# Perceiver megakernel on one core: in self attention, ScalarE copies one of four score banks to SBUF and GpSimd subtracts its maximum

## The reference

```
q = (X @ Wq.T + bq).reshape(b, s, N_KV, g, HEAD_DIM)      # 8 x 4 heads of width 8
k = (X @ Wk.T + bk).reshape(b, s, N_KV, HEAD_DIM)
v = (X @ Wv.T + bv).reshape(b, s, N_KV, HEAD_DIM)
scores = einsum('bkgqd,bkld->bkgql', q, k) / sqrt(HEAD_DIM)
weights = softmax(scores)                                   # over 64 keys
out = einsum('bkgql,bkld->bkgqd', weights, v)
x = x + out @ Wo.T + bo
```

## Time and profile before

| | |
|---|---|
| time, median of 3 runs | 3079.71 us (3079.54 to 3079.81) |
| the profiled execution, its time | 3095.65 us |
| the profiled execution, its span | 3093.9 us |
| granted TensorE clock over the span | 0.963 of full speed |
| busy, TensorE matmul | 2728.1 us (88%) |
| busy, VectorE | 1893.3 us (61%) |
| busy, ScalarE | 1381.1 us (45%) |
| busy, GpSimd | 1025.4 us (33%) |

### The profile page before, as it was taken

The page is one execution under the profiler, slowest core; times in us unless marked ns, Lnnn a source line. Parts: engine busy times, 40 slices in busy tenths (PEclk is TensorE's granted clock), DMA queues, the critical chain, the costliest instruction groups (busy, mean ns, idle before and its releaser), DMA issues. The chain is left out here.

```text
span 3093.9 us, 51159 instructions
## 1 busy us (share of the span) xinstructions
PE 2728.1 (88%) x19360; PEld 1711.5 (55%) x19364; DVE 1893.3 (61%) x2524; ACT 1381.1 (45%) x2650; POOL 1025.4 (33%) x868
## 2 busy tenths in 40 slices
PE   7999987999989988899989775578988899898898
PEld 5999953466656557333356432235643555554687
DVE  3666646222268637444478597768854899996332
ACT  3332343122257646222257553446767566652223
POOL 1222200233135322000045300015610899991462
PEclk9999999999999999999999887789999999999999
DMA  4000005111200000200000000000011112213224
GB/s 156 21 27 20 17 7 196 41 47 47 74 21 2 23 1 2 85 1 0 22 2 2 15 0 0 0 22 2 2 42 37 58 73 75 70 46 112 65 82 147
DMA packets 77016, 128.94 MB, mean 42 GB/s; under 512 B 12112, under 2 KB 54736, under 8 KB 76304
## 3 DMA queue, kind: packets, MB, share of 16 engines
q1 hardware_dynamic: 67888, 101.78, 9.9%
q0 software_dynamic: 8928, 24.39, 2.5%
HBM read 107.40 MB, written 18.74 MB: 41 GB/s over the span
## 5 line engine op out<-in xcount | busy, mean ns | idle before, releaser
L3433 POOL TENSOR_TENSOR h<-ssm_u,ss_bc 128x1024 f32<-128x1024 f32 x88 | 205.8, 2360 | 0.0
L3396 ACT ACTIVATE ssm_p_h<-ss_delta,ss_decay 128x256 f32<-128x256 f32 x352 | 146.6, 463 | 123.9 <-DVE ctxT L3470 82.9
L3343 PE MATMUL ssm_p_y<-ctxT,ident 128*128 128x512 f32 x412 | 187.8, 596 | 0.0
L3465 DVE TENSOR_TENSOR_SCAN ssm_p_h<-ssm_p_h,h 128x1024 f32<-128x1024 f32 x64 | 145.9, 2279 | 8.7 <-ACT ssm_p_h L3396 6.8
L683 POOL TENSOR_TENSOR xw_prob<-xw_prob,xw_rsum 128x512 f32<-128x512 f32 x64 | 65.3, 1041 | 259.1 <-DVE xw_rsum L632 259.1
L3423 POOL TENSOR_TENSOR ctxT<-ctxT,ss_bc 128x1024 f32<-128x1024 f32 x50 | 117.6, 2360 | 19.3 <-DVE ctxT L3463 19.3
L514 PE MATMUL xw_p_q<-h,xw_m_h 128*128 (+1 forms) x1024 | 119.7, 278 | 1.3 <-PEq L60 1.3
L514 PEld LDWEIGHTS xw_p_q<-h,xw_m_h 128*128 128x128 f32 x1024 | 116.6, 193 | 7.0 <-issue 7.0
L3343 PEld LDWEIGHTS ssm_p_y<-ctxT,ident 128*128 128x128 f32 x412 | 76.5, 192 | 79.5 <-issue 78.3
L3327 PE MATMUL ssm_p_h<-ssm_b_diagonal,ssm_uT 128*128 128x128 f32 x640 | 82.9, 284 | 39.9 <-DVE ctxT L3470 19.5
L522 PE MATMUL xw_p_q<-xw_u,xw_vo_h 128*128 128x128 f32 x1024 | 117.1, 275 | 1.2 <-ACT xw_u L586 1.2
(11 more groups left out here) (863 smaller groups left out, 7143.7 us busy)
## 6 DMA issues: line engine op xcount, KB each, us to landing
ss_bc<-ss_bc_rows SPq DMA_DIRECT2D x24, 896.0 KB, 4.3
xw_ctx_rows<-in_ctx_rows SPq DMA_DIRECT2D x32, 256.0 KB, 2.6
ss_bc<-ss_bc_rows SPq DMA_DIRECT2D x8, 768.0 KB, 4.0
L3f_rows<-L3f_rows_out SPq DMA_DIRECT2D x16, 384.0 KB, 4.0
L0f_wg<-in_L_ffn_gate SPq DMA_DIRECT2D x9, 512.0 KB, 9.4
L0f_wu<-in_L_ffn_up SPq DMA_DIRECT2D x9, 512.0 KB, 9.4
L0f_wd<-in_L_ffn_down SPq DMA_DIRECT2D x9, 512.0 KB, 9.5
L0f_rows<-L0f_rows_out SPq DMA_DIRECT2D x16, 256.0 KB, 3.9
```

Of the source, the lines that this page charges most:

```text
L3343: mm = pe.matmul(p_y[:, 2 * half:2 * half + 2, :].rearrange("p e t -> p (e t)"), k.ident[:, :], weighed[n % RING_W][:, ts(half, CH)], star ...
L3396: i = act.activation(out[:, ts(e, CT)], delta[:, e, ts(c, CT)], ACT.Exp, scale=decay[:, E4 * s + e:E4 * s + e + 1])
L3433: g.tensor_tensor(tiles(drive[n % RING]), u[:, c % 2, :, :], bcast(bcs[:, row_b(s), :], 1, E4), ALU.mult).then_inc(sem["driven_g"], 1)
L3465: v.tensor_tensor_scan(slot, factor, term, 0.0, ALU.mult, ALU.add).then_inc(sem["scanned"], 1)
```

## The change

Of the four score banks, VectorE handles three from PSUM as before. The fourth is copied by ScalarE to a new SBUF tile `raw` (`copy_raw`, one copy of 512 columns). VectorE takes its maximum from `raw` in a second reduce, and GpSimd adds the negated maximum and writes the fourth quarter of `prob` (`move`). `score(i)` now waits for `shifted` and `copied`; exp waits for `shifted` and `moved`. `nmax` gets two slots. GpSimd's `spread_q(i + 2)` no longer waits for `scored`; it stands behind `move(i)`, which waits for `copied` and `maxed`.

```diff
-            nmax = sb(k, mid, "nmax", [P, 4, 8])
+            raw = sb(k, mid, "raw", [P, 4, 2, S])
+            nmax = sb(k, mid, "nmax", [P, 2, 4, 8])
...
                 def score(i):
                     if i >= 1:
                         pe.wait_ge(sem["shifted"], i)
+                        pe.wait_ge(sem["copied"], i)
...
             def _(act):
+                def copy_raw(i, free=True):
+                    act.wait_ge(sem["scored"], i + 1)
+                    if free:
+                        act.wait_ge(sem["moved"], i)
+                    act.copy(raw[:, :, :, :], p_s[:, 3, :, :, :]).then_inc(sem["copied"], 1)
+
                 def tile(i, u, last=False):
                     act.wait_ge(sem["shifted"], i + 1)
+                    act.wait_ge(sem["moved"], i + 1)
                     act.activation(prob..., ACT.Exp, scale=scale).then_inc(sem["exped"], 1)
+                    if not last:
+                        copy_raw(i + 1)
                     for m in range(4):
...
                 def soft(i, u, free=True):
                     v.wait_ge(sem["scored"], i + 1)
-                    v.tensor_reduce(nmax[:, :, :], p_s[all four banks], ...max, negate=True).then_inc(sem["maxed"], 1)
+                    if free:
+                        v.wait_ge(sem["moved"], i - 1)
+                    v.tensor_reduce(nmax[:, u, 0:3, :], p_s[:, 0:3, ...], ...max, negate=True)
+                    v.wait_ge(sem["copied"], i + 1)
+                    v.tensor_reduce(nmax[:, u, 3, :], raw[...], ...max, negate=True).then_inc(sem["maxed"], 1)
                     v.wait_ge(sem["maxed"], i + 1)
                     if free:
                         v.wait_ge(sem["turned"], 4 * i - 4)
-                    v.tensor_tensor(prob[all four quarters], p_s[all four banks], bcast(nmax)).then_inc(sem["shifted"], 1)
+                    v.tensor_tensor(prob[:, u, 0:3, ...], p_s[:, 0:3, ...], bcast(nmax[:, u, 0:3])).then_inc(sem["shifted"], 1)
...
+                def move(i, u, free=True):
+                    g.wait_ge(sem["copied"], i + 1)
+                    g.wait_ge(sem["maxed"], i + 1)
+                    if free:
+                        g.wait_ge(sem["turned"], 4 * i - 4)
+                    g.tensor_tensor(prob[:, u, 3, ...], raw[...], bcast(nmax[:, u, 3, :], 2, S), ALU.add).then_inc(sem["moved"], 1)
...
                     for u in range(2):
-                        g.wait_ge(sem["scored"], 2 * j + u - 1)
-                        spread_q(2 * j + u, u)
+                        move(2 * j + u, u)
+                        spread_q(2 * j + u + 2, u)
```

More of the change, by code:

```diff
@@ L2024, in self_attention @@
         with ExitStack() as mid:
-            sem = semaphores(nc, mid, k.prefix, "q_spread scored maxed shifted exped turned turned_read mixed mixed_read returned recip weighed")
+            sem = semaphores(nc, mid, k.prefix, "q_spread scored copied maxed shifted moved exped turned turned_read mixed mixed_read returned recip weighed")
             qx = sb(k, mid, "qx", [P, 2, H2, 2, 4, S])
             prob = sb(k, mid, "prob", [P, 2, 4, 4, 2, S])
+            raw = sb(k, mid, "raw", [P, 4, 2, S])
             probT = sb(k, mid, "probT", [P, 4, 4, P])
             oT = sb(k, mid, "oT", [P, 4, P])
-            nmax = sb(k, mid, "nmax", [P, 4, 8])
+            nmax = sb(k, mid, "nmax", [P, 2, 4, 8])
             rsum = sb(k, mid, "rsum", [P, 4, 4, 2])
@@ L2094, in _, with tile @@
                 act.preload_act_table(ACT.Exp)
-                def tile(i, u):
+                def copy_raw(i, free=True):
[3 more added lines that the diff above has]
+                    act.copy(raw[:, :, :, :], p_s[:, 3, :, :, :]).then_inc(sem["copied"], 1)
+                def tile(i, u, last=False):
                     act.wait_ge(sem["shifted"], i + 1)
+                    act.wait_ge(sem["moved"], i + 1)
                     act.activation(prob[:, u, :, :, :, :], prob[:, u, :, :, :, :], ACT.Exp, scale=scale).then_inc(sem["exped"], 1)
+                    if not last:
+                        copy_raw(i + 1)
                     for m in range(4):
@@ L2103, in tile @@
                     act.copy(oT[:, :, :], p_m[:, :, :]).then_inc(sem["mixed_read"], 1)
-                with act.Fori(0, NT // 2) as j:
+                copy_raw(0, free=False)
+                with act.Fori(0, NT // 2 - 1) as j:
                     for u in range(2):
                         tile(2 * j + u, u)
+                tile(NT - 2, 0)
+                tile(NT - 1, 1, last=True)
             @block.vector
@@ L2112, in soft @@
                     v.wait_ge(sem["scored"], i + 1)
-                    v.tensor_reduce(nmax[:, :, :], p_s[:, :, :, :, :].rearrange("p r m b s -> p r (m b) s"), AX, ALU.max, negate=True).then_inc(sem["maxed"], 1)
+                    if free:
+                        v.wait_ge(sem["moved"], i - 1)
+                    v.tensor_reduce(nmax[:, u, 0:3, :], p_s[:, 0:3, :, :, :].rearrange("p r m b s -> p r (m b) s"), AX, ALU.max, negate=True)
+                    v.wait_ge(sem["copied"], i + 1)
+                    v.tensor_reduce(nmax[:, u, 3, :], raw[:, :, :, :].rearrange("p m b s -> p (m b) s"), AX, ALU.max, negate=True).then_inc(sem["maxed"], 1)
                     v.wait_ge(sem["maxed"], i + 1)
@@ L2116, in soft @@
                         v.wait_ge(sem["turned"], 4 * i - 4)
-                    v.tensor_tensor(prob[:, u, :, :, :, :].rearrange("p r m b s -> p (r m b) s"), p_s[:, :, :, :, :].rearrange("p r m b s -> p (r m b) s"),
-                                    bcast(nmax[:, :, :].rearrange("p r m -> p (r m)"), 2, S), ALU.add).then_inc(sem["shifted"], 1)
+                    v.tensor_tensor(prob[:, u, 0:3, :, :, :].rearrange("p r m b s -> p (r m b) s"), p_s[:, 0:3, :, :, :].rearrange("p r m b s -> p (r m b) s"),
+                                    bcast(nmax[:, u, 0:3, :].rearrange("p r m -> p (r m)"), 2, S), ALU.add).then_inc(sem["shifted"], 1)
                 def weigh(i):
@@ L2144, in spread_q @@
                     last.then_inc(sem["q_spread"], 1)
+                def move(i, u, free=True):
[3 more added lines that the diff above has]
+                        g.wait_ge(sem["turned"], 4 * i - 4)
+                    g.tensor_tensor(prob[:, u, 3, :, :, :].rearrange("p m b s -> p (m b) s"), raw[:, :, :, :].rearrange("p m b s -> p (m b) s"),
+                                    bcast(nmax[:, u, 3, :], 2, S), ALU.add).then_inc(sem["moved"], 1)
                 spread_q(0, 0)
                 spread_q(1, 1)
-                with g.Fori(1, NT // 2) as j:
+                for u in range(2):
+                    move(u, u, free=False)
+                    spread_q(2 + u, u)
+                with g.Fori(1, NT // 2 - 1) as j:
                     for u in range(2):
-                        g.wait_ge(sem["scored"], 2 * j + u - 1)
-                        spread_q(2 * j + u, u)
+                        move(2 * j + u, u)
+                        spread_q(2 * j + u + 2, u)
+                move(NT - 2, 0)
+                move(NT - 1, 1)
         k.prefix = "sao_"
```

## The result

Median of 20 runs of each kernel, taken in turn: 3078.32 us (3071.50 to 3080.89) against 3082.22 us (3079.39 to 3090.42) before. The ratio is 0.998 with a 95% interval of 0.9974 to 0.9987. In time that is 6.2 us less, between 4.0 and 8.0. The ratio isn't that of the two medians: they are 3.9 us apart, the two means 5.2, which shows how coarse a whole time is for this change. The forecast was a gain of 7.1 us (3072.6 from 3079.7), so the interval holds it; it also holds the 4.9 of the first rival. The time of 3072.6 itself can't be laid beside 3078.32: it was reckoned from the 3079.71 of three runs, and the 20 runs of the same kernel have 3082.22. It is a gain clear of the noise, but right at the 0.2% that the prediction gave as the limit of what counts.

The account below looks back on a forecast made before the run. A closed ring of scores, reduce and subtraction on single score banks was taken as the bound, 6.94 us per tile. First tile 0.47 plus 15 turns at 0.44 gave 7.1: 3079.7 to 3072.6 us, range 3070.8 to 3076.4.

Parts of the forecast that it names:

- the first rival: Attention loop: half-clock stretches no longer absorbed cost about 1.1 us each, two leave a gain of 4.9; chance 0.20.
- Two rings, A at 6.94 and B at 6.44: Per tile: A is score, reduce, subtraction, 6.94 us; B is exp, transposes with copies, `mix`, copy to `oT`, 6.44.
- The subtraction falls by 0.54, the split reduce costs 0.07: VectorE per tile: subtraction over 1536 columns instead of 2048, 2.29 to 1.75 us; two reduces 2.36 against 2.29.
- New ring A 6.50: Score to score through VectorE's reduces and subtraction: 6.50 us per tile after the change, 0.44 less; bounds 6.40 and 6.61.
- the register step: VectorE, ahead of the reduce in even tiles: taken as 0.06 us in every second tile, 0.03 on average.
- ScalarE's copy costs nothing: Between exp and the first copy to `probT`: the new 0.54 us copy is hidden, with 0.03 to 0.2 to spare.
- the hole: ScalarE's wait of 0.75 us for the first transposes, after exp; the new copy of 0.54 was to fit in it.
- GpSimd's `move` ends 0.7 before the subtraction: After the maxima: `move` ends about 1.2 us later, VectorE's subtraction 1.9 later, so exp isn't held.
- Sum 7.1: Whole gain in us: 0.47 from the first tile's two steps plus 6.6 from 15 turns at 0.44.
- The fifteen turns: Attention loop, first tile's first reduce to the last tile's: 15 turns at 0.44 us less, 6.6 forecast.
- The rival of the half clock: Attention loop: reduced-clock stretches delay exp, each costing about 1.1 us, giving 3074.8 us; chance 0.20.
- The rival of mutual holding: `move` and VectorE's subtraction exclude each other, GpSimd first: 1.04 us more per tile, 3089 us in all; chance 0.05.

Follow-up runs that it names:

- the run beside GpSimd: Against the version without GpSimd's `move` (VectorE adds the fourth bank from `raw`): `spread_q` waits for `shifted`, running beside that addition; loop 116.66 us.

## Why the prediction was right

By its own steps:

- *Two rings, A at 6.94 and B at 6.44.* Right. The earlier trace rows gave A and the profile after has B at 6.44, in every second tile, with no idle time. Both limits were then shown apart: without the copy to `oT` on ScalarE the pace stayed at 6.42 and 6.51 (A), with two banks taken off VectorE it stayed at 6.50 (B).
- *The subtraction falls by 0.54, the split reduce costs 0.07.* Measured 2.29 - 1.76 = 0.53; the reduces 1.67 + 0.68 = 2.35 to the end of the second, against 2.29: 0.06. The gain comes from the subtraction alone.
- *New ring A 6.50.* Measured 6.42 and 6.50 in turn, 6.46 in the mean. The step from the subtraction to `score` shrank from 0.15 to 0.10, which was not foreseen, and the register step cost 0.09 in even tiles where 0.06 was assumed.
- *ScalarE's copy costs nothing.* Right, and shown apart: in the kernel before it left the loop at 124.03. Its price was over-estimated (0.54, where 0.46 to 0.48 was measured) and the hole under-estimated (0.75, where 0.85 was), so the margin was wider than said.
- *GpSimd's `move` ends 0.7 before the subtraction.* It ends at 1149.96, the subtraction at 1150.58: 0.6.
- *Sum 7.1.* The loop gave 7.6, the whole time 6.2 (4.0 to 8.0). The fifteen turns gave 7.2 (103.99 to 96.80) where 6.6 was forecast; the 0.6 more is 15 x 0.04, the shorter ring A. What lies outside them gave 0.4, where 0.5 was forecast. The whole time bears out none of these terms: its interval is 4 us wide, and that 6.2 lies so near 7.1 is partly luck. It is the loop time that bears them out.
- *The rival of the half clock.* It didn't come: up to the last tile no window of the loop has a reduced clock (below, the one at 1200 us, in which the kernel before had 0.83). In the last tile both kernels have such a stretch, transposes of 3.49 us before and 3.30 after. TensorE sat idle for less before each `score`, 0.6 where it was 1.07. Why the stretches went wasn't tested; TensorE's idle time shrank and the tiles came at other times, both at once. That each would have cost 1.1 in the changed kernel wasn't seen either, as none came where ring B could pass it on.

The window at 1200 us of the changed kernel (busy times of the engines, then the clock), and its last tile's transposes.

```profile
1200.00:1210.00 10.00, 8.59 (x196) 7.38 (x196) 8.02 (x11) 7.80 (x11) 5.91 (x6) 1.00 0.01 2
```

```profile
1230.19 3.30 PE L2060 MATMUL sam_p_t<-ident,sam_prob 128*128 128x128 f32 x16 [2.52 <-ACT sam_prob L2107]
```

- *The rival of mutual holding.* It fell for this change: the subtraction with one operand in PSUM isn't held. With both in SBUF holding exists, as the run beside GpSimd showed.

What the prediction didn't say is that GpSimd is hardly needed: without it the loop took 0.2 more. It priced VectorE's relief and the earlier release of the score banks as one thing, and it is the second that counts.

## What to carry to other kernels

Where two engines wait for each other, measure the closed ring from one event to its next occurrence, and look for a second ring at a place where the first is disturbed: a half-clock stretch showed the floor of 6.44 before anything was changed, and it held. Work on a buffer counts in such a ring only up to the moment that sets the buffer free; moved behind the release, the same work on the same engine, which had idle time there, cost 0.2 us in 16 tiles. And a gain of some us in a kernel of 3 ms is seen in the stage's own time (reproducible here to 0.03 us in three pairs of executions), not in the total, which differs by 10 us between executions of one program.

## What the runs showed of the hardware that was not expected

- The spread of whole times (3079.39 to 3090.42 for the kernel before) lies outside this loop: in the profiles what lies ahead of the loop takes 1116.7 to 1122.9 us, what lies behind it 1835.6 to 1850.0, and the loop itself repeats to 0.03 in another execution of the same kernel.
- Half-clock stretches in the loop came at the same distance from its start in the executions profiled (80.8 and 101.7 us after it in both profiles of the kernel before, and also in the one with the added copy, whose loop started 1.9 us later; 108.0 in both of the changed kernel, whose loops started 2.6 us apart), not at the same time of the span.
- Copies of 512 columns from PSUM on ScalarE, each recorded at 0.58, follow each other every 0.46 to 0.48 when nothing is waited for, and the first starts 0.10 before the recorded end of exp.
- A register step between two waits of VectorE costs 0.09 us when it stands behind the wait that comes last.
